# A routed two-layer kernel on one core: x2 in three visits, the second routing a visit sooner, W2 sooner, more fillers, full fills before the last gathers

## What is computed

```
x1 = x  + 0.5 * MoE(layernorm(x))
x2 = x1 + attention(layernorm(x1))
x3 = x2 + 0.5 * MoE(layernorm(x2))

MoE(h):  e = argmax(softmax(h Wg + bg))          one of 4 experts for each token
         gelu(h W1[e] + b1[e]) W2[e] + b2[e]     128 -> 512 -> 128
attention(h):  q' = elu(h Wq' P) + 1, k' = elu(h Wk' P) + 1, v = h Wv'     P is 128 x 32
               KV = k'^T v over the row,  out = (q' KV) / (sum(q') + 1e-8)
```

## Time and profile before

| | |
|---|---|
| time, median of 3 runs | 238.57 us (235.69 to 240.69) |
| the profiled execution | 238.41 us, span 236.7 us |
| PE busy | 206.5 us, 87% |
| DVE busy | 159.3 us, 67% |
| ACT busy | 127.0 us, 54% |
| POOL busy | 160.9 us, 68% |
| mean granted clock of TensorE | 0.954 |
| granted clock, 30 to 40 us | 0.66 |
| DMA engines, 10 to 20 us, busy share | 1.00 |

### The profile page before, as it was taken

The page is one execution under the profiler, slowest core; times in us unless marked ns, Lnnn a source line. Parts: engine busy times, 40 slices in busy tenths (PEclk is TensorE's granted clock), DMA queues, the critical chain, the costliest instruction groups (busy, mean ns, idle before and its releaser), DMA issues. The chain is left out here.

```text
span 236.7 us, 6286 instructions
## 1 busy us (share of the span) xinstructions
PE 206.5 (87%) x1740; PEld 194.1 (82%) x1740; DVE 159.3 (67%) x641; ACT 127.0 (54%) x406; POOL 160.9 (68%) x226
## 2 busy tenths in 40 slices
PE   8989589797999989999988989899879899999900
PEld 7979469696999988989988987788769899999900
DVE  3699453389688989698888869588585655543400
ACT  1415046457565677545674586644573677666500
POOL 7223888854848687064137788849878888888875
PEclk9999958998899999999999999999997999999985
DMA  4997569873444462235703953415741796662111
GB/s 103 377 312 168 185 218 351 281 177 124 170 163 151 182 205 64 102 131 202 276 0 103 343 160 97 152 65 196 263 175 40 254 345 222 236 223 86 44 55 44
DMA packets 28454, 41.69 MB, mean 176 GB/s; under 512 B 7795, under 2 KB 14851, under 8 KB 28422
## 3 DMA queue, kind: packets, MB, share of 16 engines
q1 hardware_dynamic: 24448, 34.24, 41.0%
q0 software_dynamic: 3072, 6.82, 11.1%
q10 hardware_dynamic: 902, 0.23, 0.4%
HBM read 9.41 MB, written 6.82 MB: 69 GB/s over the span
## 5 line engine op out<-in xcount | busy, mean ns | idle before, releaser
L1141 ACT ACTIVATE hT<-U,slab 128x128 f32<-128x128 f32 x304 | 86.8, 371 | 56.9 <-PE U L966 56.9
L966 PE MATMUL U<-hT_in,slab 128*128 (+1 forms) x608 | 85.5, 286 | 1.5 <-ACT hT_in L1135 1.5
L977 PE MATMUL DN<-W,hT 128*128 (+1 forms) x608 | 83.9, 283 | 0.0
L966 PEld LDWEIGHTS U<-hT_in,slab 128*128 128x128 f32 x608 | 77.2, 199 | 2.6 <-issue 1.9
L977 PEld LDWEIGHTS DN<-W,hT 128*128 128x128 f32 x608 | 76.0, 197 | 1.2 <-issue 0.8
L430 POOL DMA_INDIRECT G<-rows,src x64 | 62.7, 980 | 15.2 <-issue 10.3
L731 DVE SCALAR_TENSOR_TENSOR G<-DN,mask,G 128x128 f32 (+1 forms) x76 | 26.5, 348 | 29.8 <-PE DN L977 28.3
L416 POOL MEMSET rest<- 128x512 f32 (+1 forms) x79 | 35.9, 454 | 9.8 <-DVE G L731 4.3
L442 POOL DMA_INDIRECT out_dram<-G x32 | 31.7, 992 | 7.2 <-issue 6.4
L707 DVE TENSOR_SCALAR xn<-G 128x128 f32<-128x128 f32 x64 | 25.2, 402 | 9.7 <-DMA G<-rows,src 9.7
L1135 ACT ACTIVATE hT_in<-TR 128x128 f32<-128x128 f32 (+1 forms) x44 | 14.4, 328 | 21.2 <-PE TR L957 19.4
(11 more groups left out here) (159 smaller groups left out, 219.6 us busy)
## 6 DMA issues: line engine op xcount, KB each, us to landing
slab<-W SPq DMA_DIRECT2D x76, 322.0 KB, 2.7
...
G<-rows,src POOLq DMA_INDIRECT x64, 3.0
```

The lines of the kernel that those rows point to most:

```text
L966: i = eng.matmul(U[s % 3][:, c * P:(c + 1) * P], slab[s % NSLAB][:, c * P:(c + 1) * P], hT_in[ph % 2][:, bass.ds(v * P - expert_at[s], P)] ...
L977: i = eng.matmul(DN[s % 2][:, 0:D], hT[s % NHT][:, c * P:(c + 1) * P], W2[:, bass.ds(expert_at[s] + c * NE * D, D)], start=(c == 0 and not ...
L1141: i = eng.activation(hT[s % NHT][:, c * P:(c + 1) * P], U[s % 3][:, c * P:(c + 1) * P], ACT.Gelu, bias=slab[s % NSLAB][:, F + c:F + c + 1])
```

## The change

It moves work on all engines; the arithmetic stays.

- HOT1 goes from 8 to 7: the routings inside phases 1 and 2, and with FIRST1 the gathers behind them, move a visit sooner. HOT0 goes from 4 to 5.
- The four x2 steps, one in each of visits 4 to 7, are two in visit 4 and one in each of 5 and 6. `la_kv` on DVE stands before the normalizations of visit 3.
- In phases 1 and 2 `counts` and `inverse` stand at the end of their visit on PE, behind the up projection, and `inverse` is one piece.
- Statistics of row 0 go to HBM from ACT's queue (behind six copies) and not from SP's, so W2 follows x on SP.
- `busy(10)` becomes `busy(24)`, with `busy(3)` between each of the first three transposes and its up projection.
- On POOL the powers of row 1 move from visits 1 and 2 to 3 and 4. The last 16 gathers have fills of 512 columns. Seven scatters stand in phase 2 instead of eight, so 25 instead of 24 at the end, ten of them with a fill as before.
- Normalizations of late tiles move forward in phases 1 and 2, and some statistics of phase 1 move between visits.

```diff
         NORM_LATE = (-5, -4, -3, -2, -1, 0, 1, 1, 2, 3, 4, 5, 6, 7, 8, 9)
-        NORM_EARLY = (-5, -4, -3, -2, -1, 0, 0, 1, 1, 2, 2, 3, 4, 5, 7, 9)
+        NORM_MID = (-5, -4, -3, -2, -1, 0, 0, 1, 1, 2, 2, 3, 4, 5, 7, 8)
+        NORM_EARLY = (-5, -4, -3, -2, -1, 0, 0, 1, 1, 2, 2, 3, 4, 5, 6, 6)
...
         def norms_of(ph, v):
             def at(p):
-                return NORM_EARLY if p in (1, 2) else NORM_LATE
+                return (NORM_LATE, NORM_MID, NORM_EARLY, NORM_LATE)[p]
...
-        HOT0, HOT1 = 4, 8
+        HOT0, HOT1 = 5, 7
...
-        VAR_AT = ((7, 11, 15), (7, 12, 15))
+        VAR_AT = ((7, 11, 15), (10, 12, 15))
...
         def stats_of(ph, v):
-            if ph == 1 and 8 <= v <= 12:
-                return range(GS, 2 * GS + 1) if v == 12 else ()
+            if ph == 1 and 8 <= v <= 13:
+                return {10: range(4, 7), 11: (7,), 13: (8, 9)}.get(v, ())
...
+        def store_stats(eng, b, h):
+            lo, hi = h * T // 2, (h + 1) * T // 2
+            need(eng, ln0["rstd"], 2 * b + h)
+            eng.dma_start(rows0_v[b][:, lo:hi, D:RW], MR0[b][:, lo:hi, :]).then_inc(s_rows0[b], 16)
...
             eng.dma_start(w1_v[:, :, F + NC:SW], b2.unsqueeze(0).to_broadcast([P, NE, D])).then_inc(s_w["b2"], 16)
             store_x(0, 0)
             store_x(0, 1)
-            store_stats(0, 0)
-            store_stats(0, 1)
             for e in range(NE):
                 load_w2(e)
...
+                if ph > 0 and v == 4:
+                    pow_lb(o, 0)
+                if ph == 2 and v == 4:
+                    scatter(0, 0)
+                if ph > 0 and 4 <= v < 3 + NG:
+                    pow_lb(o, v - 3)
                 if ph < B and v in VAR_AT[ph]:
                     pow_la(ph, VAR_AT[ph].index(v))
...
-            SCATTERS = {v: (v - 4,) for v in range(4, 12)}
-            DONE0, PAIRS1 = 8, 10
-            LAST1 = 2 * (V - FIRST1)
+            SCATTERS = {5: (1,), 6: (2,), 7: (3,), 8: (4,), 9: (5,), 10: (6,)}
+            DONE0, PAIRS1 = 7, 10
...
                 begun(s)
-                if v in (1, 2):
-                    pow_front(1, v - 1)
+                if v in (3, 4):
+                    pow_front(1, v - 3)
                 if v + EARLY0 < T:
-                    gather(0, 0, v + EARLY0, second=v in (1, 2))
+                    gather(0, 0, v + EARLY0, second=v in (3, 4))
                 if v == HOT0 + 2:
                     place_tiles(1)
...
-                if v != FIRST1:
+                if v not in (FIRST1, FIRST1 + 1):
                     attention_pow(1, v)
                 begun(s)
                 if v + NEXT0 < T:
                     gather(0, 1, v + NEXT0)
-                if v == HOT1 + 2:
+                if v == HOT1 + 1:
                     place_tiles(2)
                 if v >= FIRST1:
                     gather_first(1, 0, s, v - FIRST1)
-                if v == FIRST1:
+                if v in (FIRST1, FIRST1 + 1):
                     attention_pow(1, v)
...
                 s = 2 * V + v
-                if v <= FIRST1:
+                if v < FIRST1:
                     begun(s)
...
                 if v == HOT1 + 1:
                     place_tiles(3)
                 if v >= FIRST1:
-                    gather(1, 1, 2 * (v - FIRST1), columns=2 * P)
-                    gather(1, 1, 2 * (v - FIRST1) + 1, columns=2 * P)
-            gather(1, 1, LAST1, columns=2 * P)
-            gather(1, 1, LAST1 + 1, columns=2 * P)
-            for t in range(DONE0, T, 2):
-                scatter(0, t, columns=2 * P)
-                scatter(0, t + 1, second=True)
-            for t in range(T):
-                scatter(1, t, second=(t % 2 == 1 or t > PAIRS1), columns=2 * P)
+                    gather(1, 1, 2 * (v - FIRST1))
+                    gather(1, 1, 2 * (v - FIRST1) + 1)
+            for k, (b, t) in enumerate([(0, t) for t in range(DONE0, T)] + [(1, t) for t in range(T)]):
+                scatter(b, t, second=(k % 2 == 1 or (b, t) > (1, PAIRS1)), columns=2 * P)
...
@@ -844,18 +842,24 @@
                         la_z(o, NG - 1, NG)
                     if v == 3:
                         la_gt(o)
-                    if 4 <= v < 4 + NG:
-                        lb_x2(o, v - 4)
+                        la_kv(o)
+                    if v == 4:
+                        lb_x2(o, 0)
+                        lb_x2(o, 1)
+                    if v in (5, 6):
+                        lb_x2(o, v - 3)
                 r = (0, 1) if ph == 0 else (1, ph - 1)
                 hot_at = HOT0 if ph == 0 else HOT1
-                if ph < B + 1 and v == hot_at + 2:
+                if ph in (1, 2) and v == hot_at + 2:
                     route_hots(ph + 1)
-                if ph < B and v == hot_at + 4:
+                if ph < B + 1 and v == hot_at + (3 if ph == 2 else 4):
                     route_src(*r)
                 if ph == 0 and v == 0:
                     norm(0, 5)
                 for ahead in norms_of(ph, v):
                     norm(*ahead)
+                if ph == 0 and v == hot_at + 2:
+                    route_hots(1)
                 if s + RES_LEAD < 2 * B * V and not full(s + RES_LEAD):
...
                     if v == 1:
                         la_z(o, 0, NG - 1)
-                    if v == 3:
-                        la_kv(o)
                 if ph < B + 1:
                     if v == hot_at:
                         route_hot(*r)
                     if v == hot_at + 1:
                         route_slots(*r)
-                    if ph == 2 and v == hot_at + 3:
-                        route_src(*r)
...
             front_gate(NG + 3)
             load_visits(0, 0)
             eng.wait_ge(s_foldd, 6)
-            busy(10)
-            turn_in(0, 0)
-            up(0)
-            turn_in(0, 1)
-            up(1)
-            turn_in(0, 2)
-            up(2)
+            busy(24)
+            for t in range(UP_LEAD):
+                turn_in(0, t)
+                busy(3)
+                up(t)
             turn_in(0, 3)
             eng.wait_ge(s_w["w2"], 16 * NE)
...
@@ -1087,11 +1085,11 @@
                     if v == 3:
                         la_q(o)
                         la_fold(o)
-                    if 4 <= v < 4 + NG:
-                        lb_num(o, v - 4)
-                if ph < B + 1 and v == hot_at + 2:
+                    if v in (4, 5, 6):
+                        lb_num(o, (0, 2, 3)[v - 4])
+                if ph == 0 and v == hot_at + 2:
                     counts(ph + 1)
-                if ph < B and v == hot_at + 4:
+                if ph == 0 and v == hot_at + 4:
                     inverse(ph + 1, 2, 4)
                 if s + UP_LEAD < 2 * B * V:
                     up(s + UP_LEAD)
@@ -1108,8 +1106,14 @@
                         la_sum(o, 2, 4)
                     if v == 3:
                         la_kv(o)
-                if ph < B + 1 and v == hot_at + 3:
-                    inverse(ph + 1, 0, 4 if ph == 2 else 2)
+                    if v == 4:
+                        lb_num(o, 1)
+                    if v == hot_at + 2:
+                        counts(ph + 1)
+                    if v == hot_at + (3 if ph == 2 else 4):
+                        inverse(ph + 1, 0, NG)
+                if ph == 0 and v == hot_at + 3:
+                    inverse(ph + 1, 0, 2)
...
                 front_copy(k)
             front_copy(NG)
             front_copy(NG + 1)
+            store_stats(eng, 0, 0)
+            store_stats(eng, 0, 1)
             hots(0, NG - 1)
```

7 lines of the change are left out of this document (1 added, 6 removed).

## The result

| | kernel before | changed kernel |
|---|---|---|
| time, median of 20 runs each | 238.58 us (235.33 to 242.08) | 239.44 us (237.91 to 240.94) |
| ratio, 95% interval | | 1.0097 (1.0059 to 1.0136) |
| profiled execution | 238.41, span 236.7 | 240.53, span 238.8 |
| start of phase 1 | 87.75 | 88.48 |
| start of phase 2 | 141.70 | 142.48 |

What follows compares the result with a forecast made beforehand. POOL was taken to bound the end: phase 3's first gather plus its fixed program. Span 236.7 + 4.7 - 4.5 - 1.3 - 3.0 = 232.6, with 1.7 around it 234.3 us; range 230.5 to 239.0.

Steps and rivals of the forecast that it cites:

- longer program of POOL: Phase 3: longer fills before the gathers (3.4 us) and one more scatter (1.26 us) lengthen POOL's program, +4.7 us.
- phase 2, first gather: Phase 2: earlier routing and closer x2 steps start phase 3's first gather at 174.5 instead of 178.98, -4.5 us.
- phase 1: Second routing a visit sooner removes TensorE's 0.87 us wait and some 0.9 of short waits: -1.3 us, bounds 0 and -2.
- phase 0: Fillers, moved row powers and later row 1 routing together give -3.0 us, bounds 0 and -5.
- The model of the end: Phase 3: the end is its first gather plus a fixed 56.0 us POOL program plus 1.7 us for last bytes.
- wait for tile 9: Phase 0: tile 9's gather goes at 38.1 instead of 39.87, TensorE resumes at 44.7 instead of 46.72, -2.0 us.
- the half-rate piece: Phase 0: TensorE's slow-clock stretch at 58.47, about 1.4 us, may or may not return; booked with later routing at -1.0.
- the statistics: Phase 0: moving row 0's statistics from SP's queue to ScalarE's costs nothing; they land by 21 to 24.
- rival 3: Phase 0: statistics land late, at 26.9 against 22.65, delaying what follows 1 to 4 us; 235.3 to 238.5, chance 0.15.
- rival 2: Phases 2 and 3: POOL's longer program outweighs the sooner start, phase 0 gives 0; 241.2 us, chance 0.1.
- point of decision: Rival 2 decides from a first gather of phase 3 later than 174.3 us.
- Rivals 1 and 4: 1: phase 0's gains come whole, 231.6, chance 0.2. 4: phase 3's extra fills are not serial, 230.9, chance 0.05.

Runs made afterwards that it cites:

- v1: Changed kernel with 256-column gather fills, b2 split at visits 0 to 5, row 0's statistics on SP, ScalarE's phase 1 routing behind its copy: 234.89 us, 0.9905 of kernel before.
- y1: The changed kernel itself, run again in a starved group: ratio 0.9758 to the kernel before.
- z1: Changed kernel with row 1's routing a visit sooner in phase 0 (HOT0 4), its one-hots ahead of the normalizations: ratio 1.0034 to the kernel before.
- z2: Changed kernel with DVE's six steps that split b2 at visits 0 to 5 of phase 0, not 11 to 16: ratio 1.0039 to the kernel before.
- w2: Same kernel as v1, in a starved group: ratio 1.0000 to the kernel before.
- z3: Changed kernel with row 1's routing at visit 4, b2 split at visits 0 to 5, 256-column fills before all 25 tail scatters: 1.0184 of the kernel before.
- z4: z3 with row 0's statistics on SP's queue ahead of W2: ratio 1.0174 to the kernel before.
- v2: The kernel of z4 once more, in another calm group: ratio 1.0168 to the kernel before.
- x4: Changed kernel with 10 fillers instead of 24 before phase 0's first tile, none between the first three tiles: ratio 0.9898 to the kernel before, starved.
- w3: Changed kernel with ScalarE copying transposes of tiles 14 and 15 ahead of its phase 1 routing work: ratio 1.0013 to the kernel before, starved.
- w4: Changed kernel with row 0's tile 6 scatter moved from visit 10 of phase 2 into the tail: ratio 0.9999 to the kernel before, starved.

## Why the prediction was wrong

The forecast's span was 232.6, measured were 238.8. In the profiled executions the miss of 6.2 us divides over its own steps so:

| step | predicted | measured |
|---|---|---|
| longer program of POOL | +4.7 | +4.45 (60.48 - 56.03) |
| phase 2, first gather | -4.5 | -3.13 (34.15 - 37.28 behind the phase's start) |
| phase 1 | -1.3 | +0.05 (54.00 - 53.95) |
| phase 0 | -3.0 | +0.73 (88.48 - 87.75) |

**The model of the end was right** for the calm condition, which is that of the result. POOL set it, with 0.9 us of waits for data, from the first gather of phase 3 plus a program whose length the fill rows gave. In calm groups the programs of 57.4, 60.5 and 64.0 us follow the fills, and from the measured first gather v1's span comes out to a tenth.

**Phase 0 failed, and it is the largest part.** The step said that the wait for tile 9 "sets the pace", and booked its end as 2.0 us won, the half-rate piece as 1.0, and the statistics "at nothing". The wait went, and so did the half rate, but neither was time won for the phase. DVE's closings of visits 3 and 11 show where the phase stands ahead of the routing of row 1 and behind it. The kernel before, then the changed one:

```profile
43.54 0.35 DVE L731 SCALAR_TENSOR_TENSOR G<-DN,mask,G 128x128 f32 x1
67.31 0.33 DVE L731 SCALAR_TENSOR_TENSOR G<-DN,mask,G 128x128 f32 x1
...
44.37 0.35 DVE L729 SCALAR_TENSOR_TENSOR G<-DN,mask,G 128x128 f32 x1 [0.32 <-PE DN L977]
68.02 0.35 DVE L729 SCALAR_TENSOR_TENSOR G<-DN,mask,G 128x128 f32 x1
```

*Up to visit 3* the changed kernel loses 0.83 us. This is the step that costed the statistics "at nothing", and rival 3: the first gather came at 24.67 (the forecast's own mark was 23.5). With gathers 1.7 us apart, that of tile 9, which the forecast had at 38.1, went at 40.25, behind the 39.87 of before, and TensorE stood 2.43 us for tiles 6 and 7 at 41.98. The issue on ACT took 0.40 and 0.59 us, from 15.77 and 16.20, and the table of sources was ready at 22.38, so it was the landing, not the issue, that was slow, on DMA engines whose share was 1.17 from 10 to 22 us (0.94 in the kernel before). The Trainium skill, DMA: Bandwidth & Descriptors, section "Issuing engines are not separate DMA queues", says that the DMAs of all issuing engines interleave on the same 16 engines, and the trace agrees: W2 was issued from 12.86 on in place of 17.54, ahead of the statistics, and they landed later. Whether their place behind W2 or their queue does it, no run separates; the runs with them on SP's queue ahead of W2 start at 22.5 to 22.7.

*From visit 3 to visit 11* nothing is won: 23.77 us before, 23.65 now. Tiles 8 and 9 are turned at 45.95 without a wait, and the clock is 1.00 where it was 0.90; yet DVE and TensorE both work for most of the stretch in both kernels. The windows of 49.4 to 66.4 us (columns as above), before, changed, y1:

```profile
49.40:66.40 17.00, 15.03 (x127) 14.22 (x126) 14.47 (x60) 10.68 (x34) 10.12 (x15) 0.90 0.51 153
49.40:66.40 17.00, 14.08 (x129) 13.03 (x128) 14.23 (x57) 10.30 (x34) 9.98 (x14) 1.00 0.46 148
49.40:66.40 17.00, 14.74 (x139) 13.98 (x138) 15.15 (x64) 10.36 (x34) 8.91 (x12) 1.00 0.42 132
```

In the fourteen profiles that leave the split of b2 in its place this stretch took 21.1 to 24.5 us, mostly the longer the sooner it began, so a part of what was won ahead of it is given back in it. That DVE's chain of routing and norms does this fits z1, where the waits only moved, but it is not shown; the busy times alone don't tell.

*Behind visit 11* DVE's work sets the pace, and this is shown. To the start of phase 1 it took 20.4 to 20.6 us in all these fourteen profiles, of both kernels, with a TensorE wait of 1.47 at 75.64 (changed) or of 0.26 (z1). With the split moved away it took 18.0 to 18.1 (z2, w2, v1) and 19.2 to 20.0 (z3, z4, v2, whose routing is at visit 4). z2 pays 0.7 for the split ahead of visit 11 and wins 2.4 behind it, 1.7 in all. Both kernels take the same time there, so the change neither won nor lost behind visit 11, and the wait of 1.47 at 75.64 cost nothing.

The clock did hold, 1.00 from 30 to 40 us; that it would be worth nothing was right, and x4 bears it out: 0.54 there, and phase 1 started at 87.65.

**Phase 1 failed by the same mistake.** The wait of 0.87 went, as said. A new one of 1.30 came, for ACT's copy, which stood behind ACT's routing work, and the two for KM grew from 0.42 and 0.18 to 0.70 and 0.53. Taking the largest away (w3) only moved it to DVE. In 16 of 18 runs the phase took 53.9 to 54.2 us; v1 and w2, with w3's order and a sooner start, took 54.9 and 54.8. A wait removed was not a gain here. w3 shows that DVE's work for KM stands behind ACT's copy; which engine sets the 54 us as a whole stays open.

**Phase 2 had the mechanism right and the size wrong.** KV came without a wait in front of the first x2 product, the wait for POOL's power shrank from 1.54 to 0.35, and the routing ran two steps closer. The four x2 steps ended 0.9 later than the sum had them, counted from the start of the phase. The first began 0.2 later. Between the steps the sum had 0.8 us, less than the three closings of 0.35 that it names; measured were 1.5, of them 0.57 with DVE idle in front of one closing. Half of this was made up by the time the table of sources was ready: 0.4 behind the forecast's 173.7. DVE's timeline of the changed kernel, which answers to the earlier trace rows:

```profile
152.01 0.69 DVE L786 TENSOR_TENSOR KV<-S,blocks 128x512 f32<-128x512 f32 x1
...
154.04 0.69 DVE L793 TENSOR_TENSOR G<-S,G 128x512 f32<-128x512 f32 x1 [0.71 <-PE S L1034]
...
161.89 0.35 DVE L729 SCALAR_TENSOR_TENSOR G<-DN,mask,G 128x128 f32 x1 [0.57 <-issue]
...
165.66 0.27 DVE L624 TENSOR_TENSOR lgm<-lgn,G 128x64 f32<-128x64 f32 x1 [0.35 <-POOL G L406]
...
171.49 2.27 DVE L656 TENSOR_TENSOR SL<-slot_i,lane_b 128x512 bf16<-128x512 int32 x3
...
174.69 0.17 DVE L691 TENSOR_SCALAR src<-tok 128x16 int32<-128x16 f32 x1
```

The other 1.0 us of the 1.4 missing is POOL: the table was ready at 174.86, just as POOL began a scatter (its row at 174.86 above), and the gather could go 1.77 later, where the sum had 0.8 (173.7 to 174.5). w4 moved that scatter away, and the gather came 1.54 sooner.

**The other rivals.** The mechanism of rival 2 came true, the longer program against the sooner start, and so did its point of decision: the first gather had to come before 174.3 and came at 176.63. Only its reason (TensorE standing for a closing in phase 2) was minor, and its chance of 0.1 too low. The other half of its condition came true as well: phase 0 gave nothing. Rivals 1 and 4 did not happen: the pitch grew in full. Rival 1's own sum is off too: it takes 6.5 us for phases 1 and 2, where the steps give 5.8.
